# The second normalisation's emission moved behind the next tile's first GELU in a fused transformer layer on 8 cores

## What is computed

```python
def _L0_attn_ref(x, w_qkv, w_proj, b_proj):   # 16 heads of 64
    ...
    scores = jnp.einsum('bhqd,bhkd->bhqk', q, k) * hs ** (-0.5)
    p = jax.nn.softplus(scores)
    p = p * p
    ...                                       # causal mask, p / sum(p), times v, w_proj
def qat_lora_linear(x, W, b, A, B):
    Wq = fake_quant_weight(W)                 # 8 bits, one scale for the tensor
    base = jnp.einsum('bsi,oi->bso', x, Wq) + b
    lora = jnp.einsum('bsr,or->bso', jnp.einsum('bsi,ri->bsr', x, A), B)
    return base + SCALING * lora
...
x = _layernorm(x + _L0_attn_ref(x, ...), axis=-1)
# the feed-forward: 1024 -> 4096, gelu, 4096 -> 1024, both qat_lora_linear
x = _layernorm(x + _L0_ffn_ref(x, ...), axis=-1)
```

## Time and profile before

| what | us |
|---|---|
| median of the two runs | 5959.78 |
| the two runs | 5933.67 and 5985.89 |
| the profiled execution, its own time | 5932.4 |
| its span, slowest core (core 3) | 5930.7 |
| spans of the eight cores | 5915.7 to 5930.7 |
| granted TensorE clock, mean of each core | 0.662 to 0.665 of full speed |

### The profile page before, as it was taken

One profiled execution on the slowest core, in us unless ns is written; L12 is line 12 of the kernel. 1 busy time (PEld: TensorE's weight loads), 2 busy tenths in 40 slices (PEclk: granted clock), 3 DMA queues, 4 the chain that ended last, 5 costly groups with the idle time before them and its releaser, 6 DMA issues. The chain is left out here.

```text
span 5930.7 us, 51399 instructions; the slowest of 8 cores (5915.7 to 5930.7 us)
## 1 busy us (share of the span) xinstructions
PE 3266.2 (55%) x12354; PEld 1103.7 (19%) x12354; DVE 2062.0 (35%) x3584; ACT 1803.3 (30%) x2209; POOL 159.9 (3%) x134
## 2 busy tenths in 40 slices
PE   0464455555665634555556630111478878788786
PEld 0120101011002201010010000000133434344343
DVE  2234333333333343333333334888821010111101
ACT  0014463654660053626636620000011111111111
POOL 0000000000000000000000000000000000000000
PEclk9875556555557856565565555555578888888798
DMA  3210101001001101010010026111100000000000
GB/s 81 82 39 21 39 10 45 8 19 32 6 6 51 50 15 46 10 46 7 8 45 6 5 74 191 53 55 55 59 20 29 15 29 15 21 23 15 29 15 15
DMA packets 91381, 205.93 MB, mean 35 GB/s; under 512 B 16823, under 2 KB 17080, under 8 KB 91100
## 3 DMA queue, kind: packets, MB, share of 16 engines
q1 hardware_dynamic: 81820, 169.09, 9.7%
q0 software_dynamic: 9280, 33.56, 1.4%
HBM read 168.79 MB, written 33.82 MB: 34 GB/s over the span
## 5 line engine op out<-in xcount | busy, mean ns | idle before, releaser
L497 ACT ACTIVATE a_tE<-psA 128x1024 f32<-128x1024 f32 x640 | 655.4, 1024 | 797.6 <-PE psA L489 772.9
L505 DVE TENSOR_TENSOR a_p<-a_ph 128x1024 bf16<-128x1024 bf16 x640 | 443.1, 692 | 1215.0 <-ACT a_ph L502 1063.8
L930 PE MATMUL psA<-b_Wp,b_h 128*128 128x512 bf16 x2048 | 576.5, 407 | 390.9 <-DVE b_Wp L766 390.9
L502 ACT ACTIVATE a_ph<-a_tE 128x1024 bf16<-128x1024 f32 x640 | 676.0, 1056 | 61.9 <-ACT a_tE L497 2.8
L489 PE MATMUL psA<-a_Q,a_K 64*128 64x512 bf16 x1280 | 651.6, 611 | 9.3 <-DVE a_Q L455 9.3
L533 PE MATMUL psU<-a_p,a_V 128*65 128x512 bf16 x640 | 330.7, 620 | 490.2 <-DVE a_p L505 273.7
L533 PE MATMUL psO<-a_p,a_V 128*65 128x512 bf16 x640 | 330.5, 619 | 473.6 <-DVE a_p L505 267.4
L954 DVE TENSOR_SCALAR b_u<-psU 16x256 bf16<-16x256 f32 x16 | 6.6, 411 | 1185.5 <-PE psU L938 1185.5
L902 ACT ACTIVATE b_h<-psO,g_bfccol 128x256 bf16<-128x256 f32 x256 | 121.4, 474 | 856.1 <-PE psO L894 856.0
L886 PE MATMUL psO<-b_X1T,b_Wfc 128*128 128x256 bf16 x2048 | 304.8, 298 | 89.3 <-DVE b_Wfc L766 76.6
L387 PE MATMUL psA<-a_xT,a_wqkv 128*128 128x512 bf16 x512 | 129.0, 419 | 323.2 <-DVE a_xT L291 323.2
(11 more groups left out here) (90 smaller groups left out, 2832.7 us busy)
## 6 DMA issues: line engine op xcount, KB each, us to landing
g_wstg<-xT SPq DMA_DIRECT2D x128, 256.0 KB
a_xf<-x SPq DMA_DIRECT2D x32, 512.0 KB
g_bc<-recb SPq DMA_DIRECT2D x128, 128.0 KB
x1scr<-g_xo POOLq DMA_DIRECT2D x32, 512.0 KB, 4.6
b_ws<-wfcT SPq DMA_DIRECT2D x32, 512.0 KB
b_ws<-wpF SPq DMA_DIRECT2D x32, 512.0 KB
b_x1f<-x1scr SPq DMA_DIRECT2D x32, 512.0 KB
b_ws<-wfcT SPq DMA_DIRECT2D x64, 256.0 KB
```

The source lines that it names most:

```text
L497: ve = kb.op("scalar", lambda E, pp=pp: E.activation(a_tE[:, :], psA[:, pp * 1024:(pp + 1) * 1024], AF.Exp, scale=0.125), waits=[(sPE, sco ...
L502: vl = kb.op("scalar", lambda E: E.activation(a_ph[:, :], a_tE[:, :], AF.Ln, bias=1.0), waits=[(sDV, st.get("ph_sq", 0))], inc=sAC)
L505: vsq = kb.op("vector", lambda E, pp=pp: E.tensor_tensor(a_p2[:, pp * 1024:(pp + 1) * 1024], a_ph[:, :], a_ph[:, :], ALU.mult), waits=[(sA ...
L930: kb.op("tensor", lambda E, q=q, tc2=tc2, oh=oh, pp=pp, f=f: E.matmul(psA[:, q * 512:(q + 1) * 512], b_h[:, pp * 256 + tc2 * 128: pp * 256 ...
```

## The change

The epilogue of a tile is no longer emitted right behind the next tile's prologue. It is wrapped in a function `epi` and put into a list, and the list is worked off inside the next tile's loop at f == 1, that is behind fc(0) and gelu(0) and ahead of fc(1). The last tile's epilogue is emitted after the loop.

```diff
                     emit_gelu(0, fcd)
                     for f in range(1, FC):
+                        if f == 1:
+                            for epi_fn in stB["lnq"]:
+                                epi_fn()
+                            stB["lnq"] = []
                         fcd = emit_fc(f)
                         emit_proj_u2(f - 1)
                         emit_gelu(f, fcd)
...
                     if tix + 1 < len(tiles):
                         pro = tile_prologue(*tiles[tix + 1])
-                    st["ln_busy"] = stB["ln_busy"]
...
-                    last_apply = 0
-                    for tc2 in range(2):
-                        va, vo, vadds = ln_and_store(
...
-                    stB["psA_free"] = last_apply
...
+
+                    def epi(ffn_done=ffn_done, tp=tp, rows0=rows0):
...
+                        last_apply = 0
+                        for tc2 in range(2):
+                            va, vo, vadds = ln_and_store(
...
+                            last_apply = vadds
...
+                        stB["psA_free"] = last_apply
...
+                    stB["lnq"].append(epi)
+
+            for epi_fn in stB["lnq"]:
+                epi_fn()
+            stB["lnq"] = []
```

More of the change, by code:

```diff
@@ L809, in build_program @@
                 "xo_free": st["xo_free"], "sm_free": st["sm_free"],
+                "lnq": [],
             }
@@ L974, in build_program @@
                         pro = tile_prologue(*tiles[tix + 1])
-                    st["ln_busy"] = stB["ln_busy"]
-                    st["ln_busy_ac"] = stB["ln_busy_ac"]
-                    st["xo_free"] = stB["xo_free"]
-                    st["sm_free"] = stB["sm_free"]
-                    last_apply = 0
-                    for tc2 in range(2):
-                        va, vo, vadds = ln_and_store(
[L982 to L988, removed]
@@ L989, in build_program @@
-                    stB["psA_free"] = last_apply
[L990 to L993, removed]
+                    def epi(ffn_done=ffn_done, tp=tp, rows0=rows0):
+                        st["ln_busy"] = stB["ln_busy"]
+                        st["ln_busy_ac"] = stB["ln_busy_ac"]
+                        st["xo_free"] = stB["xo_free"]
+                        st["sm_free"] = stB["sm_free"]
+                        last_apply = 0
+                        for tc2 in range(2):
+                            va, vo, vadds = ln_and_store(
+                                [(psA[:, (tc2 * 2) * 512:(tc2 * 2 + 1) * 512],
+                                  [(sPE, ffn_done)]),
+                                 (psA[:, (tc2 * 2 + 1) * 512:(tc2 * 2 + 2) * 512], [])],
+                                (b_x1f, (tp * 2 + tc2) * C),
+                                (d_out, rows0 + tc2 * 128), "ln2", sqbuf=b_z)
+                            last_apply = vadds
+                            stB["x1f_free"][tp * 2 + tc2] = va
+                        stB["psA_free"] = last_apply
+                        stB["ln_busy"] = st["ln_busy"]
+                        stB["ln_busy_ac"] = st["ln_busy_ac"]
+                        stB["xo_free"] = st["xo_free"]
+                        stB["sm_free"] = st["sm_free"]
```

## The result

The changed kernel takes 5857.81 us (median of 11 runs, 5853.55 to 5883.08). The kernel before, run beside it, takes 5955.29 (10 runs). The ratio is 0.9844, 95% interval 0.9823 to 0.9865. The forecast was 5848 us with a range of 5828 to 5900, and no change by more than 2%. Both hold.

The account below looks back on a forecast made before the run. PE was taken as the bound in the feed-forward stage, waiting ahead of L918 at 15 boundaries. A gain of 5.6 us each, 84 us in all, from the profiled 5932.4 us gave 5848 us, range 5828 to 5900.

Parts of the forecast that it names:

- What bounds the kernel: Feed-forward stage: PE is the bound; its large wait ahead of L918 totals 217.8 us over 15 tile boundaries.
- Step 1: ACT at a boundary: gelu(0) runs right behind fc(0), ahead of Ln and Exp, at no cost, with some 3.4 us slack.
- Step 2: PE restart: chunk 1's second add, not its scaling, releases L918, which starts at 4660.3 instead of 4667.83.
- Step 3: PE behind the restart: the 14.3 us wait becomes 6.8 ahead of L918 and 1.5 ahead of proj(1), which starts 6.07 earlier.
- Step 4: PE clock behind the restart: hidden work is worth 3.37 us, each microsecond sooner off the half clock 0.44 more.
- two bounds: Gain per boundary: 6.2 us if the clock is up at proj(1)'s start, 4.2 if its count restarts there; weighted two to one.
- The short gap: The 1.5 us PE wait ahead of proj(1): milder than the idle time of 3 us after which the clock fell.
- Hidden anyway: Rival at the boundary: chunk 1's scaling releases L918, so the gain is 1 us each, 15 in all, 5917 us; chance 0.06.
- slower, by a late fc(0): Rival: Ln and Exp wait on fc(0) through gelu(0); fc(0) 12 us late would give 5977 us; chance 0.02.
- The clock does not help: Rival behind the restart: the clock rises late, so the gain is 51 us or less, 5881 us; chance 0.12.

Follow-up runs that it names:

- Ln at gelu(3): Changed kernel with both chunks' adds run first, gelu(1) ahead too, and all four Ln and Exp ahead of gelu(3): ratio 0.9672, tile 92.23 us.
- 205 transposes: Kernel before, with 205 extra identity transposes filling PE's idle time between fc(1) and L918 at each boundary: ratio 1.0025, tile 104.86 us.
- 60 + 40 transposes: Changed kernel with 60 extra identity transposes ahead of L918 and 40 ahead of proj(1) at each boundary: ratio 0.9826, tile 98.96 us.
- 235: Kernel before, with 235 extra identity transposes between fc(1) and L918 at each boundary: ratio 0.9965, tile 102.39 us.

## Why the prediction was right

- **What bounds the kernel.** Right. The wait ahead of L918 was on the path: it lost 7.7 us, the new wait took 1.4 back, and the tile became 5.5 shorter.
- **Step 1**, gelu(0) costs nothing and 3.4 us are to spare. Right: 3.42 us idle ahead of the load, and the two runs with a late fc(0) show it nearly used up and then overdrawn.
- **Step 2**, the second add releases L918. Right: 0.14 us behind it (0.26 was taken). Freed by the scaling instead, the gain falls to 1.2 us.
- **Step 3**, two waits of 6.8 and 1.5 us. Right: 6.7 to 7.1 and 1.3 to 1.7.
- **Step 4**, the clock. The price of 0.44 us for each microsecond was right (0.43 to 0.45). The two bounds were 6.2 and 4.2 us, and both kinds of boundary are there: on core 3 the clock is up when proj(1) starts at 7 of 15 boundaries, and rises 3.0 to 5.9 us later at 8. I had taken ten and five. On the cores without a stretch at 0.81, in both profiles of this kernel, the number is 5 to 9, never ten. So the weights were wrong, and that the mean came out is in part luck. The 14 tiles of the tile time hold seven of each kind: the working then gives (6.2 + 4.2) / 2 = 5.2 us, not the 5.6 forecast, and the tile shows 5.54, since each bound was too small. Against 105.35, the tiles of the first kind are 6.6 us shorter on average and those of the second 4.5. Of the 0.3 us between 5.2 and 5.5, 0.13 are the mean time at the half clock before (6.8 us for the 6.5 taken), 0.1 that proj(1) starts 0.1 us sooner behind the psU copy than L918 did (27.64 for 27.73), and 0.1 that the late rise comes 4.3 us behind proj(1) for the 4.7 taken. A boundary of each kind, core 3: above, L931 at 4739.64 still takes 1.86; here it takes 1.02:

```profile
4531.91 1.86 PE L919 MATMUL psA<-g_bprow,g_onesb 1*128 1x512 bf16 x4 [6.91 <-DVE g_pre L309]
...
4539.38 1.02 PE L931 MATMUL psA<-b_Wp,b_h 128*128 128x512 bf16 x4 [1.34 <-ACT b_h L903]
```

- **The short gap.** On core 3 the new gap of 1.3 to 1.7 us does not by itself bring the clock down: at the seven boundaries where it had risen 1.1 to 1.7 us ahead of proj(1), it stayed up. On other cores there are exceptions. At the first boundary of cores 1 and 2 the clock had risen 2.4 and 2.7 us ahead of proj(1), and it fell again 1.0 and 0.7 us behind proj(1)'s start, for 3.4 us. What decides between the kinds of boundary the runs don't show.
- **The total.** 84 us forecast, 82 from tile times. The 5848 us stood 10 us below the median of 5857.81. That closeness is luck: the starting value of 5932.4 is 23 us below the 5955.29 of the kernel before beside it, and the medians differ by 13 us more than the 84 forecast. Neither is a step of the sum.
- **The rivals.** "Hidden anyway" and "slower, by a late fc(0)" were each built. The first gained 1.2 us for the 1 said. The second lost 4.3 us with fc(0) 6.5 us late, where 6.5 - 3.4 = 3.1 was the working. L919 itself came 3.15 us later, so the wait was priced right; the price of the tile was too mild, since the clock's rise moved as well (0.9 us of the rest), which that working left out. "The clock does not help" is out by the tile of 102.39 us.

## What to carry to other kernels

When a small operation waits in a strict queue behind a chain that it doesn't need, moving it ahead costs nothing as long as its own input is ready sooner than the one of the operation it overtakes; look up that slack, since it becomes a new dependence. Then look at what the next waiting instruction needs: here it was one value handed on by a helper that made 5.5 us of 1.2. And try to put operations that need another activation table into the steady part of a loop with idle time on ACT, not at the boundary, where PE waits for them.

## What was not expected of the hardware

- The granted clock fell from 1.00 to 0.50 when PE had been idle for only 1.6 to 1.8 us (Ln at gelu(3), core 3, in six waits of 3.7 to 4.1 us). With 205 transposes it fell within or just behind idle times of 1.8 to 3.0 us. Yet with 60 + 40 transposes it was still up behind 2.2 to 2.7 us of idle time, and fell 1.3 to 2.3 us later, under work. Idle times of 0.2 to 0.9 us (235) were followed by no fall. So the length of the idle time alone does not tell when the clock falls.
- A third grant besides 0.50 and 1.00 appeared in the tiles of two cores of one die for some hundred microseconds: cores 6 and 7 of the changed kernel and again with 70 transposes ahead of fc(0), cores 2 and 3 of the kernel before with the same 70. The other two cores of the die showed none there. Core 7 of the changed kernel's profile, same columns as above:

```profile
5400.00:5401.00 1.00, 1.00 (x10) 0.61 (x9) 0.00 (x0) 0.00 (x0) 0.00 (x0) 1.00 0.00 0
5410.00:5411.00 1.00, 1.00 (x7) 0.44 (x6) 0.00 (x0) 0.00 (x0) 0.00 (x0) 0.81 0.00 0
```

Its tiles took 105 to 113 us then instead of 99 to 101. The Trainium skill, TensorE: Matmul & The Clock Gate, Part 1, states this level, 13/16, for a die on which three cores or more run dense matmuls, and would have it all the time here. In the traces of this case the level is the exception, and where it comes it doesn't take the whole die: core 3 of the same execution ran at 1.00 between its boundaries throughout, and so did cores 4 and 5, which share the die with 6 and 7.
